# Context keys and values, first norm and first weights merged into one stage, and the experts' output biases moved from TensorE to VectorE

## The chip, the core and the metric

The kernel runs on one core of one Trainium2 chip. The metric is the device time of a whole execution in microseconds (us); lower is better. The kernel before takes 1886.22 us (median of 3 runs, 1883.31 to 1887.39).

## What is computed

x is 8 images of 256 tokens by 256 values, float32. Four residual blocks follow one another:

```
x = x + tanh(g_xattn[0]) * cross_attention_0(layernorm(x), ctx)       # 16 query heads, 4 key heads, 8 x 64 context tokens
x = x + tanh(g_ffn[0])   * block_0(layernorm(x))                      # causal self-attention, then a mixture of experts
x = x + tanh(g_xattn[1]) * cross_attention_1(layernorm(x), ctx)
x = x + tanh(g_ffn[1])   * gated_mlp(layernorm(x))
```

In cross_attention_0 the context (512 tokens of 256) gives keys and values, K = ctx Wk + bk and V = ctx Wv + bv; each key head is scaled by 1/sqrt(mean(k^2) + 1e-6). The mixture of experts takes x' = layernorm(h) and

```
comb = top-2 softmax weights of x' w_gate        # per token, one weight for each of 4 experts
eout = gelu(x' we1[e] + be1[e]) we2[e] + be2[e]  # for each expert e
m    = sum_e comb[e] * eout[e];  block_0 = h + m
```

The term be2 is the one that the change moves: tanh(g_ffn[0]) * sum_e comb[e] * be2[e] is added either way.

## The kernel before

Rows of tokens are on the 128 partitions; R holds x, 16 tiles of 128 rows by 256 (2 tiles, T = 2, make one image). XTh and XTl hold the normed and transposed x as a high and a low part (fp32r), and every weight has the same two parts, Wh and Wl, so that a product is three matmuls (`three`, lines 572 to 576: high with high, high with low, low with high). Each part of the kernel is a phase: five engine programs, joined at the end of the phase by `phase_end` (lines 113 to 121), where all engines wait for one another and POOL clears the phase's semaphores. Inside a phase everything waits on counted semaphores in an order written out by hand. All loads are issued by SP, one queue, in the order of its program. Weights come in chunks through RAW, two buffers: `stream_sp` loads chunk c when chunk c - 2 is split, `split` (lines 139 to 148) lets POOL write its high and low part.

**The opening** has these pieces in a row. `init_sp` (line 165) loads the identity, the gates and all of x (four loads of 512 KB); `init_all` makes every engine wait for all of them. `pre_sp` (line 600) loads biases, norm weights, the mask and small tables, eleven loads, some of them broadcast to 128 partitions. Then phase `context` (line 454): three loads of 512 KB (context, Wk, Wv), then the first 8 weight chunks; TensorE makes four key tiles (L482), four value tiles (L489) and the keys' transposes (L499); for each key tile VectorE adds the bias (L510), POOL squares it (L526), VectorE sums (L514), POOL makes the inverse root (L528, L530), VectorE scales (L518), ScalarE moves the transposed keys and the values out. After its four inverses POOL splits the 8 chunks. Then phase `layer_norm` "n0" (line 189): for each image, VectorE's statistics (L249, L253), POOL's inverse root (L212, L216), VectorE's rows (L268), transposes on TensorE (L307), ScalarE's high part (L320), VectorE's low part (L274). Its loops work two images ahead: statistics of image k stand beside rows of image k - 2. The next phase, cross attention 0, begins on TensorE with the query product of L574.

**The expert stage** (`experts`, line 2055) has 32 steps c, image c // 4 and expert x = c % 4. TensorE's order is up(c + 3), down(c), and at some steps context keys (c = 2 to 5), their transposes (8 to 11), context values (13, 15, 17, 19) for the second cross attention, and at x = 2 the transposes of the next norm. up is 12 products (L2133 to L2135), down is 12 products (L574 to L576) in two halves of 128 tokens, and each half starts with a product for the bias, 2 partitions deep:

```
o = pS[:, c % 2, t * D:(t + 1) * D]                                               # 2146
e.matmul(o, ones[:, :], b2s[:, x * D:(x + 1) * D], start=True, stop=False)        # 2147
```

ScalarE takes GELU (L2238) and the hidden high part (L2242). VectorE's order at step c is low(c), the hidden low part (L2300), for which down(c) waits; combine(c - 1), which adds comb times the output to R (L2309), two operations; and then, at x = 0, gated (L2317, tanh(g) * R plus the residual row xsp) and the statistics of the next norm, at x = 1 its rows (L373), at x = 3 its low part (L2330), which waits for ScalarE's copy of the transposed rows. The residual rows were written to a spill tensor earlier and come back image by image (L2120), two buffers, loaded after the context, the tables and the mask. The bias is prepared at the start: POOL memsets (L2377 to L2380), two ScalarE copies (L2229, L2230), one VectorE operation (L2344), behind the gates' chain (`gates`, line 2271).

Of the kernel before, what the change touches and what calls it, by code (L numbers as in the profile page):

```python
# [68 lines left out]
def build(nc, d, out, spill, stop=99):  # L69
    ctx = ExitStack()  # L70
    with ctx:
# [67 lines left out]
        def split(pool, raw_in, split_hi, split_done, cw, step, s, slot):  # L139
# [13 lines left out]
        ld_R, ld_c, c_half, c_tanh, out_done = (  # L153
            lasting_sem(x) for x in ("ld_R", "ld_c", "c_half", "c_tanh", "out_done"))
# [9 lines left out]

        def init_sp(sp):
            sp.dma_start(ident[:, :], d["ident"]).then_inc(ld_c, 16)
            sp.dma_start(gates[:, :], d["gates"].partition_broadcast(P)).then_inc(ld_c, 16)
            for k in range(4):
                sp.dma_start(R[:, 4 * k:4 * k + 4, :], x_rows[:, 4 * k:4 * k + 4, :]).then_inc(ld_R, 16)

        def init_pool(pool):
            pool.memset(mhalf[:, :], -0.5).then_inc(c_half, 1)

        def init_act(act):
            act.wait_ge(ld_c, 32)
            act.activation(tanhg[:, :], gates[:, :], ACT.Tanh).then_inc(c_tanh, 1)

        def init_all(e):
            e.wait_ge(ld_c, 32)
            e.wait_ge(ld_R, 64)  # L180
            e.wait_ge(c_half, 1)
            e.wait_ge(c_tanh, 1)

        def layer_norm(name, double=False, affine=None, after=None, gate=None):


            last_round = 1 if double else 0
            s_st = [sem(f"{name}_stats{r}") for r in range(2)]
            s_rs = [sem(f"{name}_rstd{r}") for r in range(2)]
            s_bs, s_p, s_hid, s_xn, s_tr, s_af, s_hi, s_lo, s_wg = (
                sem(f"{name}_{x}") for x in ("bst", "pool", "hid", "xn", "tr", "af", "hi", "lo", "wg"))
            scope = ExitStack()
            bst = sb(name + "_bst", [P, 2, T, 6], F32, scope)
            xn = sb(name + "_xn", [P, 2, T, D], F32, scope)
            xa = sb(name + "_xa", [P, 2, KD, S], F32, scope) if affine is not None else None  # L200
            AHEAD = 2

            def columns(i):
                return slice(i * S, (i + 1) * S)

            def pool(e):
                done = 0

                def inverse(i, r):
                    nonlocal done  # L210
                    e.wait_ge(s_st[r], i + 1)
                    e.tensor_scalar(rstd[:, r, i, :], mv[:, r, i, :, 1], 1e-5, 1.0, ALU.add, ALU.mult  # L212
                                    ).then_inc(s_p, 1)
                    done += 1
                    e.wait_ge(s_p, done)
                    e.tensor_tensor(rstd[:, r, i, :], rstd[:, r, i, :], mhalf[:, 0:T], ALU.pow  # L216
                                    ).then_inc(s_rs[r], 1)

                def low(i, s):
                    e.wait_ge(s_hi, i + 1)  # L220
                    e.tensor_tensor(XTl[:, :, columns(i)], xa[:, s], XTh[:, :, columns(i)].bitcast(F32),
                                    ALU.subtract).then_inc(s_lo, 1)

                def add_after(i):
                    e.wait_ge(s_xn, i + 1)
                    e.tensor_tensor(R[:, T * i:T * i + T, :], R[:, T * i:T * i + T, :],
                                    bc(after[:, :], 1, T), ALU.add)

                for k in range(B + 2 * AHEAD + 1):
                    if k < B:  # L230
                        inverse(k, 0)
                    if double and 0 <= k - AHEAD < B:
                        inverse(k - AHEAD, 1)
                    i = k - AHEAD * (last_round + 1) - 1
                    if 0 <= i < B:
                        if after is not None:
                            add_after(i)
                        if affine is not None:
                            low(i, i % 2)
                phase_end(e, name)  # L240

            def dve(e):
                done = 0

                def stats(i, r):
                    nonlocal done
                    b = (done // T) % 2
                    for t in range(T):
                        e.bn_stats(bst[:, b, t, :], R[:, 2 * i + t, :]).then_inc(s_bs, 1)  # L249
                    done += T  # L250
                    e.wait_ge(s_bs, done)
                    for t in range(T):
                        ins = e.bn_aggr(mv[:, r, i, t, :], bst[:, b, t, :])  # L253
                    ins.then_inc(s_st[r], 1)

                def first_norm(i):
                    e.wait_ge(s_rs[0], i + 1)
                    for t in range(T):
                        ins = e.tensor_scalar(R[:, 2 * i + t, :], R[:, 2 * i + t, :], mv[:, 0, i, t, 0:1],
                                              rstd[:, 0, i, t:t + 1], ALU.subtract, ALU.mult)  # L260
                    ins.then_inc(s_hid, 1)
                    e.wait_ge(s_hid, i + 1)

                def norm(i, s):
                    e.wait_ge(s_rs[last_round], i + 1)
                    e.wait_ge(s_tr, pos(i - 1))
                    for t in range(T):
                        ins = e.tensor_scalar(xn[:, s, t, :], R[:, 2 * i + t, :], mv[:, last_round, i, t, 0:1],  # L268
                                              rstd[:, last_round, i, t:t + 1], ALU.subtract, ALU.mult)
                    ins.then_inc(s_xn, 1)  # L270

                def low(i, s):
                    e.wait_ge(s_hi, i + 1)
                    e.tensor_tensor(XTl[:, :, columns(i)], pT[:, s, :].rearrange("p (k n) -> p k n", k=KD),  # L274
                                    XTh[:, :, columns(i)].bitcast(F32), ALU.subtract).then_inc(s_lo, 1)

                for k in range(B + 2 * AHEAD + 1):
                    if k < B:
                        stats(k, 0)
                    if double and 0 <= k - AHEAD < B:  # L280
                        first_norm(k - AHEAD)
                        stats(k - AHEAD, 1)
                    i = k - AHEAD * (last_round + 1)
                    if 0 <= i < B:
                        norm(i, i % 2)
                    if affine is None and 0 <= i - 1 < B:
                        low(i - 1, (i - 1) % 2)
                phase_end(e, name)

            def pe(e):  # L290
                def logits(i):
                    e.wait_ge(s_lo, i + 1)
                    for t in range(T):
                        o = pF[:, (T * i + t) * E:(T * i + t + 1) * E]
                        for k in range(KD):
                            e.matmul(o, x_part(XTh, i, k, t).bitcast(F32), gate[:, k, :], start=(k == 0), stop=False)
                            e.matmul(o, x_part(XTl, i, k, t).bitcast(F32), gate[:, k, :], start=False,
                                     stop=(k == KD - 1))

                if gate is not None:  # L300
                    e.wait_ge(s_wg, 16)
                for i in range(B):
                    e.wait_ge(s_xn, i + 1)
                    e.wait_ge(s_lo if affine is None else s_af, pos(i - 1))
                    for k in range(KD):
                        for t in range(T):
                            ins = e.transpose(pT[:, i % 2, k * S + t * P:k * S + t * P + P],  # L307
                                              xn[:, i % 2, t, k * P:k * P + P], ident[:, :])
                    ins.then_inc(s_tr, 1)
                    if gate is not None and i:  # L310
                        logits(i - 1)
                if gate is not None:
                    logits(B - 1)
                phase_end(e, name)

            def act(e):
                def body(i, s, _):
                    e.wait_ge(s_tr, i + 1)
                    if affine is None:
                        e.activation(XTh[:, :, columns(i)], pT[:, s, :].rearrange("p (k n) -> p k n", k=KD),  # L320
                                     ACT.Copy).then_inc(s_hi, 1)
# [19 lines left out]
            return Phase(sp, pool, act, dve, pe)  # L341

# [2382 lines left out]
```

## Time and profile before

| | |
|---|---|
| median of 3 runs | 1886.22 us |
| the profiled execution | 1881.76 us |
| its span | 1880.0 us |
| TensorE busy | 1743.0 us, 93% of the span |
| VectorE busy | 1095.1 us, 58% |
| ScalarE busy | 1318.6 us, 70% |
| POOL busy | 1065.5 us, 57% |
| mean granted TensorE clock | 0.974 of full speed |

The profile takes one execution apart; its span is 1.76 us shorter than that execution's time. In its rows PE is TensorE's products and PEld its weight loads, DVE is VectorE, ACT ScalarE, SPq the loads that SP issues. A row of the timeline gives start and duration in us, engine, line, operation, what is written and read, and in brackets how long the engine had been idle and what ended that. Operations of one engine follow each other closer than their durations, since they overlap; the difference of two starts is what an operation takes of its engine.

### The profile page before, as it was taken

The page shows a single profiled execution, that of the slowest core. Times are in us where ns is not written, and L with a number is a line of the kernel's source. Part 1 is how long each engine was busy: PE and PEld are TensorE (multiplying, and loading weights), DVE is VectorE, ACT ScalarE, POOL GpSimd, SP SyncE. Part 2 cuts the span into 40 slices and gives each one's busy share as a digit, 9 for nine tenths or more (in the row PEclk, how much of TensorE's full clock was granted, in tenths as well). Part 3 has the DMA queues.
Part 4 walks back from the last instruction along what each step waited for, and adds up shares of the span by engine and source line. Part 5 has one row for each costly group of instructions (what it writes and reads, how often), then busy time and mean ns, then how long its engine had stood idle before and what let it go on. Part 6 is the DMA issues. An engine that isn't in the chain of part 4 may idle for free.

```text
span 1880.0 us, 36601 instructions
## 1 busy us (share of the span) xinstructions
PE 1743.0 (93%) x11648; PEld 1570.9 (84%) x11648; DVE 1095.1 (58%) x3073; ACT 1318.6 (70%) x4254; POOL 1065.5 (57%) x1215
## 2 busy tenths in 40 slices
PE   3499999799999999999989996999999999999798
PEld 1388888688999999999978885888888888888797
DVE  1467777757776666566765553555555555565222
ACT  1177777588888878888865444888888888888221
POOL 1433334689999889889832113445454444554454
PEclk9599999899999999999999998999999999999899
DMA  3000001210000000000002100000000000000000
GB/s 115 23 15 18 16 17 41 66 31 13 13 24 18 13 24 13 18 18 12 18 1 79 28 19 8 12 8 12 12 9 12 9 12 13 19 15 12 4 24 23
DMA packets 29392, 40.17 MB, mean 21 GB/s; under 512 B 4882, under 2 KB 18450, under 8 KB 29076
## 3 DMA queue, kind: packets, MB, share of 16 engines
q1 hardware_dynamic: 29204, 37.83, 6.8%
q8 instruction: 97, 1.59, 0.4%
q14 instruction: 91, 0.75, 0.1%
HBM read 33.63 MB, written 4.19 MB: 20 GB/s over the span
## 4 chain that ended last, share of the span: by engine, by line
PE 67%; ACT 13%; issue 5%; POOL 5%; DVE 3%; DMA 0%; POOLq 0%; SPq 0%; ACTq 0%; DVEq 0%
PE pS L1072 4%; PE pF L574 4%; ACT pA L1736 4%; PE pF L576 4%; PE pF L575 4%; PE pA L576 3%; PE pA L574 3%; PE pA L575 3%; PE pA L1063 3%; PE pA L1065 3%; PE pA L1064 3%; PE pS L744 3%; PE pF L765 3%; PE pO L1091 3%; ACT x_P L1762 2%
## 5 line engine op out<-in xcount | busy, mean ns | idle before, releaser
L574 PE MATMUL pA<-Wh,XTh 128*128 128x512 f32 (+1 forms) x512 | 222.0, 434 | 5.7 <-DVEq L117 2.9
L1482 POOL TENSOR_TENSOR f_sw<-f_sw,f_sin 128x512 f32<-128x512 f32 x128 | 181.6, 1419 | 40.8 <-ACT f_sw L1191 40.8
L576 PE MATMUL pA<-Wh,XTl 128*128 128x512 f32 (+1 forms) x512 | 189.1, 369 | 0.0
L575 PE MATMUL pA<-Wl,XTh 128*128 128x512 f32 (+1 forms) x512 | 188.0, 367 | 0.0
L1191 ACT ACTIVATE f_sw<-pA 64x512 f32<-64x512 f32 x256 | 151.5, 592 | 36.0 <-PE pA L1065 32.2
L1485 POOL TENSOR_TENSOR f_sw<-f_sw,f_RB 128x512 f32<-128x512 f32 x128 | 168.8, 1318 | 10.0
L1063 PE MATMUL pA<-XTh,Wh 128*128 128x256 f32 x512 | 163.1, 318 | 8.2 <-DMA wg<-in_w_gate 7.5
L1762 ACT ACTIVATE x_P<-x_P,x_nm 128x192 f32<-128x192 f32 (+1 forms) x256 | 127.5, 502 | 35.8 <-DVE x_nm L1878 35.8
L569 POOL TENSOR_TENSOR Wl<-RAW,Wh 128x256 fp32r<-128x256 f32 (+3 forms) x64 | 60.7, 948 | 155.3 <-ACT Wh L562 155.3
L1065 PE MATMUL pA<-XTh,Wl 128*128 128x256 f32 x512 | 145.3, 284 | 0.0
L1064 PE MATMUL pA<-XTl,Wh 128*128 128x256 f32 x512 | 145.2, 284 | 0.0
L1989 POOL TENSOR_TENSOR x_QR<-x_QR,x_t 128x512 f32<-128x512 f32 x64 | 82.0, 1281 | 101.3 <-DVE x_QR L1855 101.3
L1212 ACT ACTIVATE f_P<-f_P,f_nm 128x128 f32<-128x128 f32 (+1 forms) x256 | 114.0, 447 | 21.6 <-DVE f_nm L1351 21.4
L1770 ACT ACTIVATE x_P<-x_P,x_rs 128x192 f32<-128x192 f32 (+1 forms) x256 | 115.9, 505 | 7.3 <-DVE x_rs L1886 7.3
L574 PEld LDWEIGHTS pA<-Wh,XTh 128*128 128x128 f32 x512 | 98.2, 192 | 26.4 <-DVEq L117 3.7
L1878 DVE CUSTOM_DVE_ANT_0 x_P<-pS,x_mask,x_nrq 128x192 f32<-128x192 f32 (+1 forms) x256 | 113.3, 480 | 4.2 <-PE pS L1628 3.4
L575 PEld LDWEIGHTS pA<-Wl,XTh 128*128 128x128 f32 x512 | 98.2, 192 | 18.7
L576 PEld LDWEIGHTS pA<-Wh,XTl 128*128 128x128 f32 x512 | 97.7, 191 | 17.2
L1072 PE MATMUL pS<-f_kT,f_qT 128*128 128x128 f32 (+1 forms) x512 | 105.5, 329 | 4.9 <-POOL f_kT L1488 4.9
L1351 DVE CUSTOM_DVE_ANT_0 f_P<-pS,f_mask 128x128 f32<-128x128 f32 (+1 forms) x256 | 80.8, 353 | 47.3 <-PE pS L1072 46.4
L1063 PEld LDWEIGHTS pA<-XTh,Wh 128*128 128x128 f32 x512 | 98.1, 192 | 11.6 <-issue 7.9
L1220 ACT ACTIVATE f_P<-f_P,f_rs 128x128 f32<-128x128 f32 (+1 forms) x256 | 101.5, 447 | 2.7 <-DVE f_rs L1359 2.5
(295 smaller groups left out, 6084.4 us busy)
## 6 DMA issues: line engine op xcount, KB each, us to landing
RAW<-in_w_f SPq DMA_DIRECT2D x32, 256.0 KB, 2.6
RAW<-in_w_x SPq DMA_DIRECT2D x32, 160.0 KB, 2.2
RAW<-in_w_x SPq DMA_DIRECT2D x32, 128.0 KB, 2.0
RAW<-in_w_ff SPq DMA_DIRECT2D x8, 288.0 KB, 2.8
R<-in_x SPq DMA_DIRECT2D x4, 512.0 KB, 6.0
x_spill<-R SPq DMA_DIRECT2D x8, 256.0 KB, 2.0
RAW<-in_w_moe SPq DMA_DIRECT2D x8, 256.0 KB, 2.7
moe_xs<-x_spill SPq DMA_DIRECT2D x8, 256.0 KB, 3.1
```

The source lines that it names most:

```text
L574: e.matmul(o, ah, bh, start=first, stop=False)
L575: e.matmul(o, ah, bl, start=False, stop=False)
L576: return e.matmul(o, al, bh, start=False, stop=last)
L1063: e.matmul(o, Wh[g % 2][:, w], xh, start=(k == 0), stop=False)
L1064: e.matmul(o, Wh[g % 2][:, w], xl, start=False, stop=False)
L1065: ins = e.matmul(o, Wl[g % 2][:, w], xh, start=False, stop=(k == KD - 1))
L1072: ins = e.matmul(pS[:, h % 2, OFF[t]:OFF[t] + WID[t]], qT[:, i % 2, h, t * P:(t + 1) * P], kT[:, i % 2, h, 0:WID[t]], start=True, stop=True)
L1191: ins = e.activation(sw[dst, n, :, :], pA[src, n % 2, :].rearrange("p (a n) -> p a n", a=2), ACT.Copy)
L1482: e.tensor_tensor(y, y, bc(sind[:, :], 1, 2), ALU.mult).then_inc(q["swm"], 1)
L1485: e.tensor_tensor(y, y, RB[:, g % 2, 2 * n:2 * n + 2, :], ALU.add).then_inc(q["swb"], 1)
L1762: ins = e.activation(x, x, ACT.Exp, scale=-1.0, bias=nm[:, h, t:t + 1], accum_out=sm[:, h, t:t + 1])
L1770: ins = e.activation(x, x, ACT.Copy, scale=rs[:, h, t:t + 1])
```

## The change

The opening's five pieces become one phase, `first_stage`. Loads are issued in this order: context, Wk, key bias, identity, gates, value bias, key weights, x rows of images 0 and 1, Wv, weight chunks 0 and 1, the other x rows, query bias, mask, chunks 2 to 7, and last the norm weights and tables of later stages. Every user waits for its own load. The squares of the keys and their scaling go to ScalarE. The norm is written with one image's statistics and rows one after the other. In the expert stage the bias product goes, and VectorE adds comb times tanh(g) times be2 to the reloaded residual rows, two operations a step.

```diff
-        def init_sp(sp):
...
-        def layer_norm(name, double=False, affine=None, after=None, gate=None):
...
-        def context(name, scope, wk, wv, KT, w_col, bk=None, VT=None, bv=None, VC=None, first_stream=None):
...
+        def first_stage(name, q, norm, cT, wkv, kb, sq, ss, KT, VT, bq, bk, bv, wcol, mask):
...
+            def pe(e):
...
+                e.wait_ge(q["ck"], 32)
+                for c in range(4):
+                    keys(c)
+                e.wait_ge(q["cv"], 16)
+                values(0)
+                values(1)
+                e.wait_ge(q["id"], 32)
+                norm_tr(0)
+                values(2)
+                key_tr(0)
+                values(3)
+                norm_tr(1)
+                key_tr(1)
+                key_tr(2)
+                norm_tr(2)
+                key_tr(3)
+                for b in range(3, B):
+                    norm_tr(b)
...
+            def act(e):
+                def squares(c):
+                    e.wait_ge(q["kb"], c + 1)
+                    for h in range(NKV):
+                        x = slice(h * HD, (h + 1) * HD)
+                        ins = e.activation(sq[:, c, x], kb[:, c, x], ACT.Square, accum_out=ss[:, c, h:h + 1])
+                    ins.then_inc(q["sq"], 1)
+                def scaled(c):
+                    e.wait_ge(q["rk"], c + 1)
+                    for h in range(NKV):
+                        x = kb[:, c, h * HD:(h + 1) * HD]
+                        ins = e.activation(x, x, ACT.Copy, scale=ss[:, c, h:h + 1])
+                    ins.then_inc(q["kn"], 1)
...
+            def dve(e):
...
+                for c in range(3):
+                    take_keys(c)
+                stats(0)
+                take_keys(3)
+                stats(1)
+                rows(0)
+                rows(1)
+                for b in range(B):
+                    if b + 2 < B:
+                        stats(b + 2)
+                    low(b)
+                    if b + 2 < B:
+                        rows(b + 2)
...
+            def pool(e):
...
+                inverse(0)
+                inverse(1)
+                norm.inverse(e, 0)
+                norm.inverse(e, 1)
+                inverse(2)
+                weights(0)
+                inverse(3)
+                weights(1)
+                for b in range(2, B):
+                    norm.inverse(e, b)
+                    weights(b)
...
         def experts(scope, KT, VC, kn, tables, mask):
...
-                e.dma_start(b2[:, :], d["be2"].partition_broadcast(2)).then_inc(q["bias"], 16)
+                e.dma_start(b2[:, :], d["be2"].partition_broadcast(P)).then_inc(q["bias"], 16)
...
-                        e.matmul(o, ones[:, :], b2s[:, x * D:(x + 1) * D], start=True, stop=False)
...
+                    e.tensor_scalar(gcomb[:, :, :], comb[:, :, :], tanhg[:, 1:2], None, ALU.mult
+                                    ).then_inc(q["comb"], 1)
...
+                def bias(c):
+                    i, x = c // E, c % E
+                    if c == 0:
+                        e.wait_ge(q["bias"], 16)
+                        e.wait_ge(q["comb"], 1)
+                    if x == 0:
+                        e.wait_ge(spl[i % 2], 16 * (i // 2 + 1))
+                    else:
+                        e.wait_ge(q["xb"], T * c)
+                    for t in range(T):
+                        r = xsp[:, i % 2, t, :]
+                        e.scalar_tensor_tensor(r, b2[:, x * D:(x + 1) * D], gcomb[:, T * i + t, x:x + 1], r,
+                                               ALU.mult, ALU.add).then_inc(q["xb"], 1)
...
                     low(c)
                     if c:
                         combine(c - 1)
+                    bias(c)
```

## Rows read from the trace of the kernel before

**Rows 1.** Busy time by stretch: length, PE, PEld, DVE, ACT, POOL, PEclk, DMA share, GB/s
```profile
985.00:990.00 5.00, 4.59 (x22) 4.53 (x23) 3.49 (x11) 1.28 (x4) 0.32 (x3) 0.50 0.42 111
1099.70:1115.50 15.80, 15.80 (x110) 13.71 (x109) 8.76 (x20) 6.12 (x13) 2.20 (x4) 1.00 0.10 28
```

**Rows 2.** Timeline of the opening: start, duration, engine, line, names, idle before
```profile
10.52 0.34 SPq L601 DMA_DIRECT2D x_bq<-in_x_bq  x1
...
23.82 8.13 PE L482 MATMUL pA<-c_wkv,c_cT 128*128 128x512 f32 x12 [23.82 <-DMA c_wkv<-in_x_Wv]
...
27.61 0.69 DVE L510 TENSOR_TENSOR c_kb<-pA,x_bk 128x512 f32<-128x512 f32 x1 [8.51 <-PE pA L482]
```

**Rows 3.** Timeline of the first norm and of the first query product
```profile
71.72 0.74 DVE L249 BATCH_NORM_STATS2 n_bst<-R 128x6 f32<-128x256 f32 x2
...
73.18 0.74 POOL L216 TENSOR_TENSOR rstd<-rstd,mhalf 128x2 f32<-128x2 f32 x1
...
80.92 1.12 PE L307 MATMUL pT<-ident,n_xn 128*128 128x128 f32 x4 [0.81 <-DVE n_xn L268]
...
83.50 0.80 PE L574 MATMUL pA<-Wh,XTh 128*128 128x512 f32 x1 [1.46 <-DVEq L117]
```

**Rows 4.** Timeline of TensorE in the expert stage
```profile
1101.22 0.28 PE L2135 MATMUL pT<-XTh,Wl 128*128 128x256 f32 x1
...
1105.08 0.28 PE L2135 MATMUL pT<-XTh,Wl 128*128 128x256 f32 x1
1105.29 0.38 PE L2147 MATMUL pS<-moe_b2s,moe_ones 2*128 2x256 f32 x1
...
1105.82 0.28 PE L575 MATMUL pS<-Wl,moe_hh 128*128 128x256 f32 x1
1105.94 0.28 PE L576 MATMUL pS<-Wh,moe_hl 128*128 128x256 f32 x1
```

**Rows 5.** Timeline of VectorE in the expert stage, and its last combination
```profile
1103.50 0.69 DVE L2330 TENSOR_TENSOR XTl<-pF,XTh 128x512 fp32r<-128x512 f32 x1 [2.94 <-ACT XTh L2223]
...
1104.71 0.87 DVE L2309 SCALAR_TENSOR_TENSOR R<-pS,moe_comb,R 128x256 f32<-128x256 f32 x2
1105.68 0.75 DVE L2317 SCALAR_TENSOR_TENSOR R<-R,tanhg,moe_xs 128x512 f32<-128x512 f32 x1
...
1107.41 0.66 DVE L2300 TENSOR_TENSOR moe_hl<-pA,moe_hh 128x512 fp32r<-128x512 f32 x1
1107.99 0.87 DVE L2309 SCALAR_TENSOR_TENSOR R<-pS,moe_comb,R 128x256 f32<-128x256 f32 x2
1108.77 0.73 DVE L373 TENSOR_SCALAR n_xn<-R,mv,rstd 128x256 f32<-128x256 f32 x2
...
1119.37 0.69 DVE L2330 TENSOR_TENSOR XTl<-pF,XTh 128x512 fp32r<-128x512 f32 x1 [2.94 <-ACT XTh L2223]
...
1131.83 0.88 DVE L2309 SCALAR_TENSOR_TENSOR R<-pS,moe_comb,R 128x256 f32<-128x256 f32 x2 [1.11 <-PE pS L576]
```

**Rows 6.** Groups by line, ScalarE, 84 to 110 us: busy, mean ns, idle before
```profile
L822 ACT ACTIVATE x_sq<-x_qb 128x128 f32<-128x128 f32 x28 | 8.2, 301 | 0.4 <-issue 0.4
```

**Rows 7.** Groups by line, POOL, 23.7 to 63.3 us
```profile
L147 POOL TENSOR_TENSOR Wl<-RAW,Wh 128x256 fp32r<-128x256 f32 x8 | 6.1, 763 | 0.6
...
L530 POOL TENSOR_TENSOR c_ss<-c_ss,mhalf 128x4 f32<-128x4 f32 x4 | 4.1, 1014 | 0.3
```

**Rows 8.** Timeline around the expert stage's start and near 1093, and one load's landing
```profile
981.88 1.09 PE L381 MATMUL pT<-ident,f_RB 128*128 128x128 f32 x4 [3.41 <-DVE f_RB L373]
...
991.90 0.43 SPq L2120 DMA_DIRECT2D moe_xs<-x_spill  x1
...
995.06 0.38 PE L2147 MATMUL pS<-moe_b2s,moe_ones 2*128 2x256 f32 x1 [0.28 <-DVE moe_hl L2300]
...
1092.75 1.27 DVE L373 TENSOR_SCALAR n_xn<-R,mv,rstd 128x256 f32<-128x256 f32 x2
...
moe_xs<-x_spill SPq DMA_DIRECT2D x2, 256.0 KB, 7.3
```

More of the change, by code:

```diff
@@ L178, in init_all @@
[L178 to L182, printed above, removed]
-        def layer_norm(name, double=False, affine=None, after=None, gate=None):
[L192 to L321, printed above, removed]
-                    else:
-                        w, b = affine
-                        e.wait_ge(s_lo, pos(i - 1))
-                        for k in range(KD):
-                            ins = e.activation(xa[:, s, k, :], pT[:, s, k * S:(k + 1) * S],
-                                               ACT.Identity, scale=w[:, k:k + 1], bias=b[:, k:k + 1])
-                        ins.then_inc(s_af, 1)
-                        e.wait_ge(s_af, i + 1)
-                        e.activation(XTh[:, :, columns(i)], xa[:, s], ACT.Copy).then_inc(s_hi, 1)
-                in_order(e, B, body)
-                phase_end(e, name)
-            def sp(e):
-                if gate is not None:
-                    e.dma_start(gate[:, :, :].rearrange("p k e -> p (k e)"), d["w_gate"]).then_inc(s_wg, 16)
-                phase_end(e, name)
-            close_phase(name)
-            scope.close()
-            return Phase(sp, pool, act, dve, pe)
@@ L954, in cross_attention_0 @@
             close_phase(name)
-            return Phase(pre_sp, None, pre_act, pre_dve, None), first, norm, Phase(sp, pool, act, dve, pe)
-        pre0, context0, n0, cross0 = cross_attention_0()
+            return opening, Phase(sp, pool, act, dve, pe)
+        opening, cross0 = cross_attention_0()
         x0.close()
@@ L2079, in experts @@
             comb = sb("moe_comb", [P, NB, E], F32, scope)
-            b2 = sb("moe_b2", [2, E * D], F32, scope)
-            b2h = sb("moe_b2h", [2, E * D], F32R, scope)
-            b2s = sb("moe_b2s", [2, E * D], F32R, scope)
-            row = sb("moe_row", [2, 1], F32, scope)
-            one = sb("moe_one", [2, P], F32, scope)
-            ones = sb("moe_ones", [2, P], F32R, scope)
+            gcomb = sb("moe_gcomb", [P, NB, E], F32, scope)
+            b2 = sb("moe_b2", [P, E * D], F32, scope)
             cT = sb("c1_cT", [P, KD, 512], F32, scope)
@@ L2226, in act @@
                 e.activation(lg[:, :, :], lg[:, :, :], ACT.Exp).then_inc(q["ex1"], 1)
-                e.wait_ge(q["bias"], 16)
-                e.wait_ge(q["row"], 2)
-                e.activation(ones[:, :], one[:, :], ACT.Copy)
-                e.activation(b2h[:, :], b2[:, :], ACT.Copy).then_inc(q["b2h"], 1)
                 e.wait_ge(q["v"], 13)
@@ L2620, in _ @@
         def _(pe):
[L2621 to L2623 removed]
+            opening.tensor(pe)
             cross0.tensor(pe)
```

307 lines of the change are left out of this document (143 added, 164 removed).

## The prediction

> **What bounds the kernel now.** I read three views. First, busy times by stretch: in the middle of the expert stage TensorE works 15.80 of 15.80 us at a granted clock of 1.00, VectorE 8.76 [rows 1]. Second, the timeline of the opening: TensorE gets its first product at 23.82 and is released by a load, while the x rows, which only the norm needs, had gone first and were landed by 10.52 [rows 2]; POOL splits weights after the keys, then the norm runs alone, and the first query product starts at 83.50 [rows 3]. Third, the timelines of TensorE and VectorE in one image of the expert stage [rows 4, 5]. So the opening is bound by loads and by a chain of small steps, the experts by TensorE alone.
>
> **Opening.** The old stage goes whole, 83.5 us. The new one, in time from the start:
>
> Loads. By 10.52 some 2.1 MB were in [rows 2], so the 1 MB of context and Wk, now first, takes about 6 us: 5 at best, 8 if the loads behind share the engines with it. I take 6.2 for TensorE's start.
>
> Keys. The first key tile took 3.8 us from its start to the addition of its bias (23.82 to 27.61 [rows 2]), and the clock is cold again. So bias additions at 10.0, and with two tiles cold and two warm at 12.9, 14.6 and 16.3. Squares are now four ScalarE operations of 0.30 us [rows 6], 1.2 a tile: done at 12.0, 14.9, 17.2. VectorE's statistics of images 0 and 1 are ready at 16.3 and 18.0.
>
> POOL is then the serial engine. A key inverse is a power of 1.01 us [rows 7] with a small operation before it, 1.3 in all; a norm inverse about 1.0; a weight split 1.15 (0.76 [rows 7] and a cast, put at half of it). In its order: key 0 and 1 (16.3), norm 0 (17.4), norm 1 (19.1), key 2 (20.4), split 0 (21.5), key 3 (22.8), split 1 (24.0), norm 2 (25.0). Image 2's rows are written at 25.8.
>
> From there the norm is a chain: the new VectorE order has statistics and then rows of the same image, with POOL between, where the old code worked two images ahead. Statistics start to inverse end took 2.20 (71.72 to 73.18 + 0.74 [rows 3]), a pair of rows 0.73 (the operation at 1108.77 [rows 5]); with a little less POOL disturbance I take 2.85. Images 3 to 7: 25.8 + 5 x 2.85 = 40.0. From the last image's transposes to the first query product took 2.6 (80.92 to 83.50 [rows 3]): 42.6. Values, key transposes and splits lie beside this (last split 40.4). SP is moved past by all of it: the six small loads that it issues last land near 41.7 and are late next. POOL then clears some 20 more semaphores, an estimated 1.5 us, hidden, since its first result is needed later by ten.
> 83.5 - 42.6 = **-40.9**. Bounds for the end: 37 (POOL waits less) and 50 (loads at 8, 3.4 a norm image).
>
> **Experts: removed.** Each of 64 bias products (L2147, 2 partitions deep) stands between products of 128. Ordinary ones follow at 0.12 (1105.82 to 1105.94); from the last up product over the bias product to the second down product are 0.74 (1105.08 to 1105.82), where 0.24 would do [rows 4]. That is 0.50 each, 32 us in all, and TensorE's 15.87 an image (1103.50 to 1119.37 [rows 5]) would be 11.87.
> By the Trainium skill ("TensorE: Matmul & The Clock Gate", Why this matters for your kernels) a lone product with a small contraction takes the time of a full one. The sum would then be 64 x 0.12 = 8 us; the rows show four times that, and the trace does not agree.
> The bias row's own preparation on VectorE and ScalarE goes too, and a small scaling comes. The first GELU waits for the gates' second exponential, not for these, so I count nothing: the gate chain hides them, and a microsecond is what they would cost bare.
>
> **Experts: added.** 64 additions of 128x256 on VectorE. The nearest row is the combination, whose two operations of this shape take 0.78 together (1107.99 to 1108.77 [rows 5]). Bounds: 0.36 each (half of 0.73 above) and 0.64 (half of the 1.27 below); I take 0.79 a pair. VectorE per image, starts to starts [rows 5]: norm low with low part 1.21, three more low parts 1.8, four combinations 3.16, gating and statistics 1.73, rows 0.65, and now four bias pairs 3.16: 11.7. TensorE and VectorE become equal, and waits decide:
> a) The norm's low part waits for ScalarE and comes 2.28 after the last up product (1101.22 [rows 4] to 1103.50 [rows 5]), the next expert's low part right after it, 1.21 both. The next down product can then start 3.5 after the one before, not 2.85: 0.66 lost.
> b) In the following step VectorE has combination, bias pair, gating, statistics and low part, 0.79 + 0.79 + 1.73 + 0.60 = 3.91 against 2.85: 1.06 lost.
> So 1.72 an image of the 4.0. Images 4 and 5 have context value products on TensorE that cover it, the first ones context keys; step by step the first 27 experts lose 5.1.
> c) Tail: after expert 28 no up products stand between. VectorE alone has 11.1 from the combination of expert 27 to that of 31 by the terms above; the old time is 1119.37 + 1.21 to 1131.83 [rows 5], 11.25. The last five experts' ten bias products gain nothing: 5.0 less.
> d) Head: the first addition waits for the first reload of residual rows, which was needed four experts later. It was issued at 991.90 and took 7.3 [rows 8], so 999.2; the bias rows for 128 partitions put 512 KB ahead of it instead of 8, 0 to 1.5 us, I take 0.7. Behind this wait on VectorE stands the low part of expert 1, and for that TensorE's down product: 999.9 + 0.87 + 0.7 = 1001.5. TensorE is ready at 995.06 [rows 8] + 2.86 = 997.9: 3.6 lost. After an idle 3.41 before 981.88 [rows 8] the products ran at a granted 0.50 from 985 to 990 [rows 1], which is 1.2 GHz; the same here is about 2.0 more.
> 32 - 5.1 - 5.0 - 3.6 - 2.0 = **-16.3**. Bounds: -27 (only c) and +3 (R4).
> By the Trainium skill ("SBUF — State Buffer", Who interferes with whom) a VectorE operation with two SBUF inputs, as the additions are, and a GpSimd operation that reads SBUF block each other. One pair of the rows operation took 1.27 instead of 0.73 (1092.75 [rows 8]), beside a POOL split, so the trace knows such meetings; one an image would be 4 us less gain. POOL has but 2.20 us in 15.8 [rows 1].
>
> **Sum.** The profiled execution took 1881.8 (span 1880.0). 1881.8 - 40.9 - 16.3 = 1824.6. The runs' median is 4.4 above it, so I expect 1829.0 of the runs. Under 0.2% (3.8 us) a difference could not be told from none.
>
> **Rivals**, all from the median 1886.2.
> R1, VectorE keeps pace: a, b and d do not show, only the tail is lost: -40.9 - 27 = 1818.3. For: VectorE idles 7 of 15.8 us now [rows 1]. Against: the 2.28 and the 1.21 stand in line whatever the additions cost. 14%.
> R2, VectorE is the bound: additions at 0.64, so b loses 1.56, the step after it 0.55, with a 2.77 of 4.0. 8 x 1.23 - 5.6 at the head = -4.2: 1841.1. For: loads of 11.7 and 11.87 are equal. 15%.
> R3, the opening gives only 30, loads slowing each other and a norm image at 3.4: 1839.9. 7%.
> R4, a bias product cost no more than its 0.12: 8 us go, and 5.1 + 3.6 + 2.0 come. 1886.2 - 40.9 + 2.7 = 1848.0. Against: rows 4 repeat at every expert. 3%. The first page named above would have it so.
> R5, slower, by the price of the additions. At p each an image takes 8.55 + 8p on VectorE, eight images 64p - 58.6 more than now; that eats the opening when p is above 1.55 us, four times the combination's. At 1.9: 1886.2 - 40.9 + 63.0 = 1908.3. Nothing in the trace has such a price at this width. 2%.
> R6, no change: later phases give it back. Against: nothing works across the phase's end before 83.50. 1%.
>
> **Numbers.** Forecast 58%: 1829.0, by itself 1819 to 1838. The range takes in R1, R2 and R3: 1809 (R1 with an opening of 37 and some of the tail) to 1847. Faster by more than 0.2% 0.97, same 0.01, slower 0.02.
>
> **What would show it.** Key product at 6, image 2's rows near 26 and then one image each 2.85, first query product at 42.6. In the experts no L2147, an image of 13.6 without context work, TensorE waiting on the hidden low part at two experts of four, an idle time near the first reload with a half clock behind it. It is wrong if an image takes 11.9 (R1) or 15 (R2), or if the first query product comes after 50.

## The result, and the profile after

The changed kernel takes 1832.9 us (median of 4 runs, 1829.1 to 1833.7) where the old one takes 1886.4: ratio 0.9715, 95% interval 0.9698 to 0.9733. That is 53.5 us less, faster, against a forecast of 1829.0 with a range of 1809 to 1847. The profiled execution took 1833.7 (span 1831.9), at the upper end of its own runs, while the profiled one of before lay 4.6 below its median; so the two spans differ by 48.1 only. This is where they come from:

| part of the span | before | after | difference | forecast |
|---|---|---|---|---|
| start to the first query product | 83.50 | 45.63 | -37.9 | -40.9 |
| from there to the gates' first operation (untouched code) | 902.73 | 907.18 | +4.4 | 0 |
| from there to the last combination's start | 145.60 | 131.81 | -13.8 | -16.3 |
| from there to the end | 748.17 | 747.28 | -0.9 | 0 |

Busy times by stretch of the kernel after, for [rows 1]: near the expert stage's head, one image of it without context work, and the stage's tail. The columns are length, PE, PEld, DVE, ACT, POOL, PEclk, DMA share, GB/s.

```profile
967.70:971.20 3.50, 3.50 (x19) 3.50 (x19) 3.38 (x8) 0.00 (x0) 2.93 (x5) 0.51 0.00 0
1056.90:1070.70 13.80, 12.52 (x102) 11.97 (x101) 11.87 (x28) 6.14 (x14) 2.22 (x4) 1.00 0.12 33
1078.00:1082.00 4.00, 3.31 (x16) 3.23 (x16) 3.15 (x8) 0.00 (x0) 0.00 (x0) 0.50 0.00 0
```

An image now has 11.87 us of VectorE in 13.80 (8.76 in 15.80 before), and TensorE, once full, has gaps: 12.52 of 13.80. Behind its first 5 us, which were slow before too [rows 1], TensorE runs twice at about half its clock in the stage.

The timeline of the opening, for [rows 2, 3]:

```profile
5.88 10.16 PE L345 MATMUL pA<-c_wkv,c_cT 128*128 128x512 f32 x16 [5.88 <-DMA c_wkv<-in_x_Wk]
...
9.70 0.69 DVE L445 TENSOR_TENSOR c_kb<-pA,x_bk 128x512 f32<-128x512 f32 x1 [1.99 <-PE pA L345]
...
16.08 0.69 DVE L445 TENSOR_TENSOR c_kb<-pA,x_bk 128x512 f32<-128x512 f32 x1
...
25.16 1.20 DVE L189 TENSOR_SCALAR n_xn<-R,mv,rstd 128x256 f32<-128x256 f32 x2 [3.48 <-POOL rstd L184]
...
31.64 0.40 POOL L145 CAST Wh<-RAW 128x256 fp32r<-128x256 f32 x1
31.80 1.20 DVE L189 TENSOR_SCALAR n_xn<-R,mv,rstd 128x256 f32<-128x256 f32 x2 [0.60 <-POOL rstd L184]
32.12 0.72 POOL L147 TENSOR_TENSOR Wl<-RAW,Wh 128x256 fp32r<-128x256 f32 x1
...
45.63 0.79 PE L285 MATMUL pA<-Wh,XTh 128*128 128x512 f32 x1 [1.46 <-DVEq L117]
```

TensorE starts at 5.88 (forecast 6.2), the bias additions run from 9.70 to 16.08 (10.0 to 16.3), and image 2's rows, begun at 25.16, are written at 26.36 (25.8). From there an image takes 3.32 us where I had 2.85, five times over: the pair of rows takes 1.20 instead of 0.73, from image 2 on, and each time a POOL cast has begun just before it.

The expert stage: its head, one image, and its tail, for [rows 4, 5, 8]:

```profile
958.55 0.43 SPq L2022 DMA_DIRECT2D moe_xs<-x_spill  x1
...
965.07 1.35 DVE L2222 SCALAR_TENSOR_TENSOR moe_xs<-moe_b,moe_gcomb,moe_xs 128x256 f32<-128x256 f32 x2 [3.48 <-DMA moe_xs<-x_spill]
...
967.07 0.39 PE L285 MATMUL pS<-Wh,moe_hh 128*128 128x256 f32 x1 [2.35 <-DVE moe_hl L2197]
...
1054.77 0.28 PE L285 MATMUL pS<-Wh,moe_hh 128*128 128x256 f32 x1
...
1056.94 0.69 DVE L2242 TENSOR_TENSOR XTl<-pF,XTh 128x512 fp32r<-128x512 f32 x1 [1.82 <-ACT XTh L2122]
...
1058.28 0.39 PE L285 MATMUL pS<-Wh,moe_hh 128*128 128x256 f32 x1 [0.49 <-DVE moe_hl L2197]
...
1062.16 0.38 PE L285 MATMUL pS<-Wh,moe_hh 128*128 128x256 f32 x1 [0.79 <-DVE moe_hl L2197]
...
1075.95 0.39 PE L285 MATMUL pS<-Wh,moe_hh 128*128 128x256 f32 x1 [2.23 <-DVE moe_hl L2197]
...
1084.62 0.88 DVE L2206 SCALAR_TENSOR_TENSOR R<-pS,moe_comb,R 128x256 f32<-128x256 f32 x2 [0.62 <-PE pS L287]
```

All the waits that I named are there: the reload at the head with TensorE's idle 2.35 behind it, and in each image a wait behind the norm's low part (0.49, wait a) and one in the next step (0.79, wait b). From one down product's start to the next are 3.51 us with wait a (1054.77 to 1058.28) and 3.88 with wait b (to 1062.16). The two norm low parts at 1043.38 and 1056.94 are 13.56 apart (forecast 13.6), those at 1056.94 and 1070.73 13.79. The groups by line of the whole stage show the change of roles. Before, VectorE idled 41.0 us waiting for down products ahead of its combinations:

```profile
L2309 DVE SCALAR_TENSOR_TENSOR R<-pS,moe_comb,R 128x256 f32<-128x256 f32 x64 | 27.9, 478 | 41.0 <-PE pS L576 41.0
```

After, it is 8.9, and TensorE waits 11.1 us for VectorE:

```profile
L285 PE MATMUL pS<-Wh,moe_hh 128*128 128x256 f32 x128 | 38.8, 303 | 11.1 <-DVE moe_hl L2197 11.1
L2222 DVE SCALAR_TENSOR_TENSOR moe_xs<-moe_b,moe_gcomb,moe_xs 128x256 f32<-128x256 f32 x64 | 28.8, 491 | 3.5 <-DMA moe_xs<-x_spill 3.5
L2206 DVE SCALAR_TENSOR_TENSOR R<-pS,moe_comb,R 128x256 f32<-128x256 f32 x64 | 27.8, 474 | 8.9 <-PE pS L287 8.8
```

### The profile page after: what moved, and what is told of

Same layout as the page of the kernel before. It is cut to its first block, busy times and chain, and to the rows that moved or that the text cites. A ratio compares the mean times of both kernels' runs of the same rounds, so it can differ in the third digit from the quotient of the medians.

```text
span 1831.9 us, 36545 instructions
## 1 busy us (share of the span) xinstructions
PE 1717.3 (94%) x11584; PEld 1559.8 (85%) x11584; DVE 1118.2 (61%) x3129; ACT 1327.2 (72%) x4300; POOL 1064.2 (58%) x1208
## 4 chain that ended last, share of the span: by engine, by line
PE 65%; ACT 14%; issue 6%; POOL 5%; DVE 4%; DMA 1%; SPq 0%; POOLq 0%; ACTq 0%; DVEq 0%
PE pS L978 4%; PE pF L285 4%; ACT pA L1642 4%; PE pF L287 4%; PE pF L286 4%; PE pA L287 4%; PE pA L285 4%; PE pA L286 3%; PE pA L969 3%; PE pF L671 3%; PE pA L971 3%; PE pA L970 3%; PE pS L650 3%; PE pO L997 3%; ACT x_P L1668 3%
## 5 line engine op out<-in xcount | busy, mean ns | idle before, releaser
L286 PEld LDWEIGHTS pA<-Wl,XTh 128*128 128x128 f32 x512 | 98.0, 191 | 18.7
```

The lines of the kernel that those rows point to most:

```text
L286: e.matmul(o, ah, bl, start=False, stop=False)
```

## The experiments

Below, "the stage" is the time from the gates' first operation to the start of the last combination (145.6 before, 131.8 after), and "an image" the distance of two norm low parts without context work between them (15.87 before, 13.6 to 13.8 after).

**Each half alone.** First the new opening with the old function `experts`:

> The new opening with the old expert stage (the bias products stay on TensorE). Theory: the parts add up. The first query product starts at 45.6 us as in the changed kernel (83.5 before), later phases start 38 earlier, and the time is 38 below before: ratio about 0.980 (1848). Rival A (part of the opening is given back in cross attention 0, where the changed kernel lost 4.4 us against before at its end, as a consequence of the new start): ratio 0.982, and the step-by-step difference there falls from 38 to about 34 again at steps 29 to 31. Rival B (the opening carries all of the gain and the experts none): 0.9715.

Measured: 1848.3 us, ratio 0.9797 (0.9784 to 0.9809). First query product at 44.98, the stage 145.58 and an image 15.86, as before. Then the old opening with the new `experts`:

> The old opening with the new expert stage (bias additions on VectorE). Theory: the expert stage from the gates' first operation to the last combination takes 132 us instead of 145.6, the time is 14 below before, ratio 0.9926 (1872.4). Rival A (the full 16.3 that I forecast is there and hidden in the changed kernel by the clock of its run): 0.991. Rival B (the expert stage gives nothing alone): 1.000.

Measured: 1872.4, ratio 0.9926 (0.9912 to 0.9941), the stage 129.99. The halves multiply to 0.9725, inside the interval of the whole. They add up, and neither is given back; the gain of the experts alone is small, but its interval lies below 1.

The +4.4 us between them belongs to neither. From the first query product to the gates, where all kernels here have the same code, the profiled executions took 902.6 to 907.2 us: 902.7 before, 907.2 after, 904.5 with the old opening and the new experts, 906.4 with the new opening, 902.6 and 903.4 in two other runs below that have the new opening too. Before and after part in two places. About 2 us come at the end of cross attention 0, where after shows a granted clock of 0.50 in 327 to 329 us and before 1.00 at the same step (363 to 365); about 2 more come 90 us later, where after shows 0.52 in 418.7 to 421.7 and before 1.00 (456.6 to 459.6). Rival A of the first run would have had it always with the new opening, and it is not. Why the clock falls in one execution and not in another stays open.

**What the additions cost.** `bias(c)` taken out of VectorE's order, so that the output biases are missing from the result:

```
-                    e.wait_ge(q["xb"], T * E * (i + 1))
+                    e.wait_ge(spl[i % 2], 16 * (i // 2 + 1))
...
-                    bias(c)
```

> The changed kernel without the 64 bias additions: the experts' output biases are left out of the result, and the gating waits only for the reload of the residual rows. Theory (waits b and d are the additions' doing, a is not): an image without context work takes 11.9 + 0.66 = 12.5 us instead of 13.6, the wait for the first reload at the head goes (about 3.5), the tail is shorter by about 4 (five pairs of 0.79): in all some 12 below the changed kernel, 1821. Rival A (the low part's chain alone holds TensorE back, the additions run beside it): an image stays at 13.6, and only head and tail gain, about 4 to 7 us. Rival B (VectorE contention with GpSimd is the price): like the theory, but rows and low parts become shorter too, 15 us or more.

Measured: 1822.8, ratio 0.9662 (0.9648 to 0.9675); the stage 121.3, an image 13.0. TensorE's waits in one image:

```profile
1047.75 0.39 PE L285 MATMUL pS<-Wh,moe_hh 128*128 128x256 f32 x1 [0.49 <-DVE moe_hl L2197]
1051.04 0.38 PE L285 MATMUL pS<-Wh,moe_hh 128*128 128x256 f32 x1 [0.20 <-DVE moe_hl L2197]
```

Wait a is the same 0.49 with and without additions, wait b falls from 0.79 to 0.20. So the 28.8 us of additions cost 10.5 us of the stage, and most of that at its ends: 4.1 up to the first norm low part and 3.7 from the combination of expert 27 on, the slow clock in both included. In a middle image they cost 0.5 to 0.8. My theory for this run had an image at 12.5: it left out that combination, gating, statistics and low part without a bias pair are still 3.12 us by the prediction's terms, longer than TensorE's 2.85. The step took 3.29 (1047.75 to 1051.04).

**Where the 0.50 us of a bias product is.** The new opening with the old experts, the bias product 128 partitions deep instead of 2:

```
-            b2 = sb("moe_b2", [2, E * D], F32, scope)
+            b2 = sb("moe_b2", [P, E * D], F32, scope)
...
-                e.dma_start(b2[:, :], d["be2"].partition_broadcast(2)).then_inc(q["bias"], 16)
+                e.wait_ge(q["row"], 1)
+                e.dma_start(b2[0:2, :], d["be2"].partition_broadcast(2)).then_inc(q["bias"], 16)
...
+                e.memset(b2[:, :], 0.0).then_inc(q["row"], 1)
```

and likewise for its high and low parts and the ones.

> The new opening and the old expert stage, but the bias product is 128 partitions deep instead of 2: rows 2 to 127 of the bias operand are zero, and the ones fill 128 partitions. The 64 products stay on TensorE, no additions on VectorE. Theory (the 0.50 us that each cost is the change of contraction depth between products of 128, twice): a bias product costs 0.12, an image 11.87 + 0.96 = 12.8 us, the stage 24 us less than with the old product: 83.5 to 45.6 for the opening and 24 here, 1886 - 38 - 24 = 1824, ratio 0.967, some 9 below the changed kernel. Rival A (the 0.50 belongs to a first product of a group, or to its weights from a tile just of ones, whatever its depth): as with the new opening alone, 1848, an image stays at 15.9. Rival B (without those 0.5 us pauses the low parts of VectorE and ScalarE come late, wait a): an image 13.5, 1829.

Measured: 1829.1, ratio 0.9696 (0.9682 to 0.9709), with all bias products still on TensorE. Its timeline there, against the 0.74 from the last up product to the second down product in [rows 4]:

```profile
1043.25 0.28 PE L2042 MATMUL pT<-XTh,Wl 128*128 128x256 f32 x1
1043.37 0.28 PE L2054 MATMUL pS<-moe_b2s,moe_ones 128*128 128x256 f32 x1
1043.48 0.28 PE L285 MATMUL pS<-Wh,moe_hh 128*128 128x256 f32 x1
1043.61 0.28 PE L286 MATMUL pS<-Wl,moe_hh 128*128 128x256 f32 x1
...
1056.50 0.39 PE L2054 MATMUL pS<-moe_b2s,moe_ones 128*128 128x256 f32 x1 [0.28 <-DVE moe_hl L2207]
```

0.36 now: a bias product is a product like the others, at 0.12. The 0.50 was the price of its depth of 2 between products 128 deep, not of one product more. Whether the depth itself is dear or the change of depth, no run here separates, since each old bias product stands between deep ones. The Trainium skill ("TensorEngine Tiling (Array Packing)", Key Properties) says that TensorE has to drain when its tiling mode changes; that the old product was in another mode no row says, but its records read 2*128 where the others read 128*128, and the runs agree with the rule. The stage is 127.5 instead of 145.6. That is 18.1, more than the 13.8 of the change, but not the 24 of my theory: an image takes 13.46 and not 12.8, since wait a (0.28 here) stays, as Rival B had it, and TensorE waits at the ends. The whole is at least as fast as the changed kernel (its interval, 0.9682 to 0.9709, overlaps the other's, 0.9698 to 0.9733): operands filled up to 128 partitions do what 28.8 us of VectorE do.

**The head.** In the changed kernel, the first reload of residual rows issued ahead of all other loads of the stage:

```
+                e.dma_start(xsp[:, 0], spill[:, 0:T, :]).then_inc(spl[0], 16)
                 e.dma_start(b2[:, :], d["be2"].partition_broadcast(P)).then_inc(q["bias"], 16)
```

> The changed kernel with the expert stage's first reload of residual rows issued ahead of the bias rows, the context and the other loads of that stage instead of behind them. Theory (the head loss is that wait and the clock that falls behind it): VectorE's idle 3.48 us before the first addition goes, TensorE's idle of 2.35 us and the half clock behind it too, the stage takes 128.3 us instead of 131.8, ratio to before 0.970, 1829. Rival A (TensorE would idle there in any case, since the low parts and additions line up behind the gate chain): 131, no difference to the changed kernel. Rival B (the saving is used up by the waits of later images, because VectorE sets their pace): head shorter, last combination the same.

Measured: 1826.3, ratio 0.9678 (0.9665 to 0.9692), the stage 125.9. The first addition:

```profile
959.20 0.87 DVE L2224 SCALAR_TENSOR_TENSOR moe_xs<-moe_b,moe_gcomb,moe_xs 128x256 f32<-128x256 f32 x2
```

No wait, and 0.87 instead of the 1.35 that it took beside POOL's table operations. Until the fifth norm low part 4.1 us are won (100.0 instead of 104.1 from the stage's start), and 1.7 more at the tail, where TensorE kept its full clock this time (12.24 from the sixth norm low part to the last combination, 13.89 in the changed kernel). That second part I had not foreseen. It does not come back in the other runs below that have this edit and the additions, except the last; whether it follows from the edit or from the execution stays open.

**Wait a.** In the changed kernel the norm's low part moved behind the norm's rows of the next image:

```
                         elif c % E == 1:
                             norm_rows(i)
-                        elif c % E == 3:
-                            norm_low(i)
+                            if i:
+                                norm_low(i - 1)
...
+                norm_low(B - 2)
```

> The changed kernel with one move: the norm's low part in the expert stage stands in VectorE's order behind the norm's rows of the next image (second expert's turn) instead of ahead of the next hidden low part (fourth expert's turn); additions, loads and opening as in the changed kernel. Theory (wait a is the order on VectorE, and the moved low part finds room in the second expert's turn): TensorE's wait of 0.49 us at the first down product of each image goes, an image without context work takes 12.9 us instead of 13.6, the stage about 128.5 instead of 131.8 in spite of the head, ratio 0.970, 1829. Rival A (VectorE's sum of 11.7 us with the combination's waits sets the pace): 13.6 stays, 1833.

Measured: 1825.6, ratio 0.9697 (0.9684 to 0.9710), the stage 125.4, an image 12.7 and 12.4. TensorE's waits in one image of it:

```profile
1059.05 0.38 PE L285 MATMUL pS<-Wh,moe_hh 128*128 128x256 f32 x1 [0.32 <-DVE moe_hl L2197]
...
1068.04 0.38 PE L285 MATMUL pS<-Wh,moe_hh 128*128 128x256 f32 x1 [1.22 <-DVE moe_hl L2197]
```

Of the two waits of an image, 0.32 is left, behind the low part in its new place; the 0.79 of the gating step is gone. The 1.22 belongs to the tail, where the up products have run out and the changed kernel waited 2.23. So wait b went too, where my theory had only wait a go, and the stage came 3.1 under its 128.5. VectorE was not the pace of the image: with the same operations in another order it does one in 12.4. By the whole time the gain is less, 3.4 us (0.9697 for 0.9715), and the two intervals overlap by 0.0012; it is the stage that shows it.

**The norm of the opening.** Statistics of image b+3 before the rows of b+2:

```
+                stats(2)
                 for b in range(B):
-                    if b + 2 < B:
-                        stats(b + 2)
+                    if b + 3 < B:
+                        stats(b + 3)
```

> The changed kernel with VectorE's statistics in the opening's norm one image further ahead of the rows (statistics of image b+3 before the rows of b+2), so that POOL's inverse no longer stands in the chain of each image. Theory (the 3.32 us of a norm image are a chain over two engines): VectorE's own work decides, 0.74 + 0.25 + 0.66 + 0.73 to 1.20 = 2.4 to 2.85 us an image, images 3 to 7 end 2.4 to 4.6 earlier, the first query product comes at 41.0 to 43.2 instead of 45.6. Rival A (POOL's inverse and split, 2.1 us, with VectorE's operations blocking each other are the pace): period 3.1 to 3.3, gain under 1. In the whole time 1829, ratio 0.9695, by the theory.

Measured: 1823.8, ratio 0.9664 (0.9651 to 0.9678), first query product at 38.86, 6.8 earlier. Some 1.3 of it is not the edit's: image 0's rows begin at 16.37 instead of 17.63, and other runs with the unchanged opening scatter as much (16.5 to 17.8). The rows of two images follow at 2.2:

```profile
29.05 0.79 DVE L189 TENSOR_SCALAR n_xn<-R,mv,rstd 128x256 f32<-128x256 f32 x2
...
31.28 0.78 DVE L189 TENSOR_SCALAR n_xn<-R,mv,rstd 128x256 f32<-128x256 f32 x2
...
34.97 1.20 DVE L189 TENSOR_SCALAR n_xn<-R,mv,rstd 128x256 f32<-128x256 f32 x2
```

The remaining 5.5 are more than the 2.4 to 4.6 that I gave it. Once POOL's inverse is out of the chain, three of the six pairs no longer meet a cast (0.79 and 0.78), and the last image follows at 1.48, since its statistics are done earlier.

**Whether POOL is why the rows take 1.20.** The changed kernel with POOL's splits 2 to 7 put after all norm inverses, a measurement and no improvement:

```
                 for b in range(2, B):
                     norm.inverse(e, b)
+                for b in range(2, B):
                     weights(b)
```

> The changed kernel's opening with POOL's weight splits 2 to 7 put behind all norm inverses; nothing else. This is to measure, not to gain: the phase ends with the last split, so the first query product should come later than 45.6. Theory (VectorE's rows take 1.20 us a pair because POOL's cast and low part run beside them and both read SBUF): the pairs of images 3 to 7 take 0.73, and a norm image 2.85 us, as I forecast. Rival A (rows are 1.20 because they come right behind POOL's power, or because of TensorE or ScalarE reading the same buffers): still 1.20 and 3.3 us.

Measured: 1831.8 us, a single execution. The rows:

```profile
30.12 0.74 DVE L189 TENSOR_SCALAR n_xn<-R,mv,rstd 128x256 f32<-128x256 f32 x2 [0.59 <-POOL rstd L184]
...
32.97 0.73 DVE L189 TENSOR_SCALAR n_xn<-R,mv,rstd 128x256 f32<-128x256 f32 x2 [0.59 <-POOL rstd L184]
...
38.52 0.40 POOL L145 CAST Wh<-RAW 128x256 fp32r<-128x256 f32 x1
38.67 1.20 DVE L189 TENSOR_SCALAR n_xn<-R,mv,rstd 128x256 f32<-128x256 f32 x2 [0.59 <-POOL rstd L184]
38.99 0.72 POOL L147 TENSOR_TENSOR Wl<-RAW,Wh 128x256 fp32r<-128x256 f32 x1
```

0.73 to 0.74 and an image in 2.85, as forecast, for every image without a split beside it; 1.20 for the last one, which has it. The first query product comes at 49.63, since the splits end later.

**Combinations.** The deep bias product with the norm ahead and the norm's low part later:

> Three things on the new opening: the norm's statistics one image ahead as in the run before; the 128-deep bias product on TensorE in the expert stage; and there the norm's low part moved from the fourth expert's turn to the second expert's turn of the next image, behind the norm's rows, so that it no longer stands between ScalarE's high part and the next hidden low part. Theory: an image takes 12.8 us (TensorE alone) instead of 13.46, the stage 127.5 - 6 x 0.66 = 123.5, the opening 3.5 less: 1829 - 4 - 3.5 = 1821.5, ratio 0.966. Rival A (wait a only moves to the step with gating and statistics): the stage stays at 127, 1825.5. Rival B (the opening gives nothing, as in Rival A of the run before): 1825.

Measured: 1819.9, ratio 0.9644 (0.9629 to 0.9659); the stage 125.1 (theory 123.5), an image 12.4 to 12.7. Wait a is gone and not moved: in the images without context work TensorE shows no wait until the tail, and Rival A is out. The order of VectorE was dear with the bias products on TensorE as well. And the changed kernel with all three repairs, the additions kept on VectorE:

> The changed kernel, bias additions on VectorE kept, with the three repairs together: first reload first, norm statistics one image ahead in the opening, the norm's low part in the experts moved to the second expert's turn. Theory: opening 3.5 less, head 3.5 less, an image 0.66 less in six images: 1833 - 11 = 1822, ratio 0.966, equal to the version with deep bias products. Rival A (VectorE, with 11.7 us of work an image, has no slack to use, so the moved low part only moves the wait): an image stays at 13.6 and the whole is 1826.

Measured: 1814.5, ratio 0.9616 (0.9602 to 0.9629); first query product 38.97, the stage 121.5, an image 12.9 and 12.4. This is the least of all, under my sum of 1822 too; its interval meets that of the version before it at 0.9629. I had 11 us for the three repairs; alone they gave 5.9 (head), 6.4 (wait a) and 6.8 (opening) of the profiled opening and stage, and together 17.0 of the 19.1. The 1.7 that the first of them had at its tail is not in the sum: from the combination of expert 27 to that of 31 it took 11.0 us there and 12.6 here. By whole times the three gave 7.0, 3.4 and 9.6 us alone and 18.7 together. Once more:

> The version with three repairs once more, on the same chip as the run beside it, so that the two are compared with each other: ratio to before 0.9616 as measured for it, within 0.0015.

Measured: 1812.8, ratio 0.9616 (0.9601 to 0.9632). Beside it, a version in which ScalarE writes the high parts of the opening's weights:

```
-                    split(e, raw_in, q["hi"], q["split"], CW_X0, c, c % 2, 0)
+                    low_w(e, q["hi"], q["split"], CW_X0, c, c % 2, 0)
```

with `high_w` in ScalarE's order ahead of each norm high part.

> The last version (three repairs, additions on VectorE), with one more edit in the opening: ScalarE writes the high parts of the weight chunks (POOL's casts go) and POOL only the low parts. Theory (it is POOL's cast, which starts just before VectorE's rows, that makes a pair of rows 1.20 us instead of 0.73): all pairs of rows take 0.73 to 0.80, the first norm images come 0.8 earlier since POOL has two casts less before them, and the first query product starts at 37.0 to 38.2 instead of 39.0; the whole 1 to 2 us less, 1813. Rival A (POOL's low part does it as well): the pairs that were 1.20 stay at 1.20, since the low part now starts where the cast did, and the opening is less than 0.5 shorter. Rival B (ScalarE becomes late with the norm's high parts): first query product at 40 or later.

Measured: 1816.7, ratio 0.9628 (0.9613 to 0.9644), no gain: the first query product comes at 44.04 instead of 39.88. Rival B is right, and Rival A for three of the six pairs, which take 1.05 to 1.16, while the other three take 0.73 to 0.74. POOL now waits for ScalarE, and where its low part meets the rows it lengthens them nearly as its cast did:

```profile
34.90 1.15 DVE L189 TENSOR_SCALAR n_xn<-R,mv,rstd 128x256 f32<-128x256 f32 x2 [0.45 <-POOL rstd L184]
35.18 0.72 POOL L280 TENSOR_TENSOR Wl<-RAW,Wh 128x256 fp32r<-128x256 f32 x1 [0.38 <-ACT Wh L273]
```

## Why the prediction was right, and where it was not

**Opening, -37.9 for -40.9.** The order of events up to image 2 was right to 0.6 us (rows written at 26.36 for 25.8). The term that was mis-sized is the norm image, "2.85 us with a little less POOL disturbance": 3.32 was measured. The 0.47 by which a pair of rows is longer comes five times there and once in image 2, 2.8 of the 3.0 missing. The row that told it was in my hands, 1.27 instead of 0.73 near 1093 beside a split [rows 8], and in POOL's new order a split follows every inverse, so the meeting comes each time. With the splits out of the way 2.85 came out exactly, so the cause is shown.

**Experts, -13.8 for -16.3.**
The 32 us of 64 bias products at 0.50 stand: in one run the products are 128 deep and cost 0.12, and R4 is out.

Waits a and b: an image of 13.56 to 13.79 for 13.6. Each was right by itself: where 2.85 is the step without a wait, 3.51 and 3.88 are 0.66 and 1.03 lost, for 0.66 and 1.06 forecast; the idle times of 0.49 and 0.79 that the rows show are only part of that. But not all of it was the additions' doing, since an image loses 1.15 without them too. Their price in a middle image is 0.5 to 0.8.

The term that was too small is the waits of the other images, and it hid behind a slip of counting. When the combination of expert 27 starts, 56 bias products lie behind it, 28.0 us, and between it and the last combination stand the eight of four experts, 4.0 us. I took 54 and the ten of five experts, 27 and 5.0. The gain at that start is 15.2 (134.3 us from the stage's start before, 119.1 after), so the waits took 28.0 - 4.1 (the head) - 15.2 = 8.7 us, not 5.1. The steps between down products say where: the six from expert 7 to expert 13, in most of which context keys are transposed, lost 4.7, and 3.9 of that without the additions too. I had counted the context's work as cover for the first images.

The head was put at 3.6 + 2.0 and cost 4.1, by the run without it. The slow clock behind it was not there in every execution. It did not fall with the old opening (stage 129.99), nor in the run with the splits last (130.1), after TensorE's idle times of 2.07 and 2.41; it fell in the changed kernel and in the run with the norm ahead (131.8 and 132.3), after 2.35 and 2.99, and in the run on wait a, after 2.13.

The tail, the last four experts, gained nothing as forecast, and lost 1.4 besides (12.7 us for 11.25), after TensorE's idle 2.23 before 1075.95, with a clock of 0.50 in 1078 to 1082.

Measured by these terms: 32 - 8.7 - 4.0 - 1.4 - 4.1 = 13.8, where I had 32 - 5.1 - 5.0 - 5.6 = 16.3. That the head came 1.5 cheaper and the tail was counted 1.0 too dear made up for 2.5 of the 5.0 missed in the waits and the clock of the tail; this part of the agreement is luck.

**The rivals.** R1 (VectorE keeps pace) and R2 (VectorE is the bound) are both wrong: an image took neither 11.9 nor 15, and the same VectorE work in another order needs 12.4. R3 took up the right cause, 3.4 for a norm image, but its loads were not slow. R6 (no change) and R5 (slower) are out by the time itself. R5's price of an addition, above 1.55 us, never came near: 0.49.

**The sum.** Of spans the forecast was -57.2 and the measured -48.1; 5.5 of this miss are the two parts above, 4.4 the untouched middle, where executions of the same code scatter by 4.6 us, less 0.9 at the end. The medians, which even this out in part, differ by 53.5, for 57.2 forecast.

## What to carry to other kernels

Before an operation is moved to another engine because it is dear, ask whether it is the operation or its shape among its neighbours: 64 small products went from 0.50 to 0.12 us each by filling their operands with zeros to the depth of their neighbours, with no work for another engine. A term for an engine's load (11.7 us against 11.87) says little until the order is laid out: what stands between one engine's result and the next step's first need decided, and moving one operation by two steps, one load by nine places or one statistic by one image gave 5 to 7 us each of the profiled stretch that it touched (3 to 10 by whole times), where the whole move to VectorE gave 13.8. Where a chain runs over two engines image by image, the disturbance that a row shows once comes in every image: count it each time.

## What the hardware showed that I had not expected

VectorE's rows operation, with one SBUF tile as input, is lengthened by POOL as much as an addition, which has two (a pair of these took 0.87 us alone and 1.35 beside POOL): a pair of rows takes 0.73 us alone, 1.20 where a cast of POOL has begun 0.15 us before, 1.15 where POOL's subtraction begins 0.28 us after it, 0.79 where only the end of that subtraction is beside it. The Trainium skill ("SBUF — State Buffer", Who interferes with whom) counts such scalar operations among those that can take the ports shared with GpSimd; the traces agree that they lose by it. The sentence that I used in the prediction, on operations with two SBUF inputs, was the less important one here: the additions, which have two, took 491 ns each on the mean against 474 for the combinations, which read one of theirs from PSUM.
